# A four-stage LayerNorm and matmul kernel: the stores of prepared weight slabs are issued by SyncE in place of GpSimd

## The chip, the cores and the metric

The kernel runs on the eight cores of one Trainium2 chip. Every core runs the same program on its own 2048 rows of the activations; weights, mask and bias are the same for all. The metric is the device time in microseconds (us) of the slowest core. The kernel before takes 3483.27 us, the median of three runs (3479.4 to 3487.8).

A core has five instruction queues: TensorE (PE) for matmuls, VectorE (DVE), ScalarE (ACT), GpSimd (POOL) and SyncE (SP). Each runs its instructions in the order in which they are written and stops at a wait for a semaphore until that is reached. DMA transfers are issued by SP and by POOL here; SP's go through queue q1 of the profile, POOL's through q0.

## What is computed

```python
# x: (2, 8192, 4096) float32; weights (4096, 4096)
block_mask  = mask.reshape(128, 32, 128, 32).sum(axis=(1, 3)) > 0     # per 32x32 block
w_masked    = L0_attn_weight * repeat(repeat(block_mask, 32), 32)
x = x + layernorm(einsum('bsk,nk->bsn', layernorm(x), w_masked))      # layer 0
bin_weight  = sign(L0_ffn_weight)
x = x + layernorm(einsum('bsi,oi->bso', layernorm(x), bin_weight) + bias)   # layer 1
```

## The kernel before

**Tiling.** The 2048 rows of a core are worked in four chunks of 512 rows (loop over `c`), a chunk through layer 0 and then layer 1. A weight matrix is cut into 16 slabs of 2048 by 512 (`sl` from 0 to 15): slab `sl` has output columns of block `nsl = sl // 2` and the half `kh = sl % 2` of the inputs. A slab in bf16 is 2 MB and stands in one of two buffers WSL. For one slab TensorE does 64 matmuls (L465), 16 for each of the four row tiles.

**Chunk 0 prepares the weights.** The slabs come as float32 in eight quarters (name of the code; eight pieces of 512 KB) through two buffers WST: SP issues the load of piece `u` when piece `u - 2` has been used (L350 to L359). In layer 0 VectorE multiplies each piece by the block mask BTE and writes bf16 (L384); in layer 1 ScalarE takes the sign (L398). When all eight pieces of a slab are done, the slab is also written to DRAM (c1m, c2m; L405 to L413). Chunks 1 to 3 then load finished slabs of 2 MB from there on SP's queue (L424). A buffer WSL is written again only when the matmuls on it and its store are done (`free_marks`); chunk 1 waits for the store of the slab that it loads.

**The mask blocks.** In chunk 0, layer 0, the mask is reduced block by block (`emit_mask_chain(nsl)`, eight blocks, each for the two slabs of one `nsl`). POOL loads four pieces of 2 MB of the int32 mask (L240, into OS for even blocks and XP for odd ones), and halves each with five adds (L255). ScalarE copies the result to COLRED (L271), TensorE sums over partitions (L283), VectorE compares with zero (L297, "the mask step" below), TensorE transposes (L288), VectorE copies to BT (L301). POOL then sends BT to DRAM (btd, L314) and from there, replicated, to one of two BTE buffers (L323), after waiting that the multiplies with the block two before are done.

**What sets the order.** The order of the program text. Blocks 0 and 1 stand before everything else. In the loop over slabs, the preparation of slab `sl + 1` stands first, then the matmuls of slab `sl`, and after those of an even slab the mask block `sl // 2 + 2`. So VectorE has, in its order, the multiplies of slab 1, the mask step of block 2, the multiplies of slab 2, evictions, the multiplies of slab 3, the mask step of block 3, and so on. On POOL each store waits for the last multiply of its slab (`wt(g, ready)`).

The line in the loop that calls the function that is changed is `nxt = emit_w_load_prep(c, layer, sl + 1)`.

Of the kernel before, what the change touches and what calls it, by code (L numbers as in the profile page):

```python
# [37 lines left out]
def build():  # L38
# [11 lines left out]
    cm_d = [nc.dram_tensor("c1m", [NSL, 128, KTS * 512], BF16, kind="Internal"),  # L50
            nc.dram_tensor("c2m", [NSL, 128, KTS * 512], BF16, kind="Internal")]
# [3 lines left out]
    with es:  # L55
# [33 lines left out]
        def inc(ins, n, k=1):  # L89
            cnt[n] += k  # L90
            ins.then_inc(sem[n], k)
            return (n, cnt[n])

        def wt(eng, marker):
            if marker is None:
                return
            n, v = marker
            if v > 0:
                eng.wait_ge(sem[n], v)

        blk = es.enter_context(nc.Block())
# [227 lines left out]
        def emit_w_load_prep(c, layer, sl):  # L329
            su = state["slab_uses"]  # L330
            state["slab_uses"] += 1
            buf = WSL[su % 2]
            nsl, kh = sl // 2, sl % 2
            free_marks = []
            if su >= 2:
                free_marks.append(slab_done.get(su - 2))
                free_marks.append(cachew_use.get(su - 2))

            if c == 0:
                q_load = {}  # L340
                L1B = NSL * NQ

                @blk.sync
                def _(s):
                    for q in range(NQ):
                        u = state["wst_uses"]
                        state["wst_uses"] += 1
                        prior = u - 2
                        if prior >= 0:
                            if prior >= L1B:  # L350
                                s.wait_ge(sem["vW2"], prior - L1B + 1)
                            else:
                                s.wait_ge(sem["vW"], prior + 1)
                        sn = "sW%d" % (u % 2)
                        s.dma_start(WST[u % 2][:, :],
                                    (w1s_d if layer == 0 else w2s_d)[
                                        sl, :, q * 1024:(q + 1) * 1024]
                                    ).then_inc(sem[sn], 16)
                        cnt[sn] += 16  # L359
                        q_load[q] = (sn, cnt[sn])  # L360
                wfirst = state["wst_uses"] - NQ

                res = {}
                if layer == 0:
                    @blk.vector
                    def _(v):
                        for q in range(NQ):
                            wt(v, q_load[q])
                            if q == 0:
                                wt(v, bte_ready[nsl])  # L370
                                for fm in free_marks:
                                    wt(v, fm)
                            j0 = q * KTQ
                            dst = buf[:, j0 * 512:(j0 + KTQ) * 512].rearrange(
                                "p (j nb i) -> p j nb i", j=KTQ, i=32)
                            src = WST[(wfirst + q) % 2][:, :].rearrange(
                                "p (j nb i) -> p j nb i", j=KTQ, i=32)
                            mk = BTE[nsl % 2][:, (kh * 16 + j0) * 16:
                                              (kh * 16 + j0 + KTQ) * 16
                                              ].rearrange("p (j nb) -> p j nb",  # L380
                                                          j=KTQ
                                              ).unsqueeze(3).broadcast_to(
                                              [128, KTQ, 16, 32])
                            ins = v.tensor_tensor(dst, src, mk, op=OP.mult)  # L384
                            inc(ins, "vW", 1)
                        res["m"] = ("vW", cnt["vW"])
                        if kh == 1:
                            bte_freed[nsl] = ("vW", cnt["vW"])
                else:
                    @blk.scalar  # L390
                    def _(s):
                        for q in range(NQ):
                            wt(s, q_load[q])
                            if q == 0:
                                for fm in free_marks:
                                    wt(s, fm)
                            j0 = q * KTQ
                            ins = s.activation(buf[:, j0 * 512:(j0 + KTQ) * 512],  # L398
                                               WST[(wfirst + q) % 2][:, :], AF.Sign)
                            inc(ins, "vW2", 1)  # L400
                        res["m"] = ("vW2", cnt["vW2"])

                ready = res["m"]

                @blk.gpsimd  # L405
                def _(g):
                    wt(g, ready)
                    sn = "sC%d" % (su % 2)
                    g.dma_start(cm_d[layer][sl, :, :], buf[:, :]
                                ).then_inc(sem[sn], 16)  # L410
                    cnt[sn] += 16
                    cachew_use[su] = (sn, cnt[sn])
                    cachew_data[(layer, sl)] = (sn, cnt[sn])  # L413
            else:
                res = {}

                @blk.sync
                def _(s):
                    for fm in free_marks:
                        wt(s, fm)  # L420
                    if c == 1:
                        wt(s, cachew_data[(layer, sl)])
                    sn = "sWs%d" % (su % 2)
                    s.dma_start(buf[:, :], cm_d[layer][sl, :, :]  # L424
                                ).then_inc(sem[sn], 16)
                    cnt[sn] += 16
                    res["m"] = (sn, cnt[sn])
                ready = res["m"]

            return ready, su  # L430
# [366 lines left out]
        for c in range(NCH):  # L797
# [11 lines left out]
            for layer in range(2):  # L809
# [21 lines left out]
                for sl in range(NSL):  # L831
# [10 lines left out]
                    ready, su = pend  # L842
# [60 lines left out]
```

## Time and profile before

| | before |
|---|---|
| median of 3 runs | 3483.27 us |
| the profiled execution, its time | 3484.26 us |
| its span (core 1, the slowest of 3453.5 to 3482.7) | 3482.7 us |
| TensorE matmul busy | 2034.3 us (58%) |
| VectorE, ScalarE, GpSimd busy | 807.0, 607.7, 342.5 us |
| moved by DMA | 573.14 MB, mean 165 GB/s |
| granted TensorE clock, mean of a core | 0.809 to 0.816 |

"Span" is from the first to the last instruction of a core, so a little under the time of the execution. "Busy" is the time in which an engine worked on an instruction; an engine that is idle waited for something, and the views of waits say for what. The page's chain that ended last gives 37% of the span to TensorE and 33% to DMA; the latter is mostly loads of w1s, w2s and mask, all in chunk 0. In the page's 40 slices TensorE is busy for 1 to 3 tenths up to slice 12 and for 5 to 9 tenths after slice 14. So the first third of the span is a stage of another kind than the rest, and is read by itself.

### The profile page before, as it was taken

The numbers are of one execution on the slowest core, as the hardware profiler recorded it, in microseconds if no ns is written. First come the engines' busy times: TensorE is split into PE (matmuls) and PEld (weight loads), VectorE is DVE, ScalarE is ACT, GpSimd is POOL, SyncE is SP. The second block draws the span as 40 slices with busy tenths as digits, with TensorE's granted clock in tenths as the row PEclk, the third lists the DMA queues.
The fourth block names the chain that finished last, engine by engine and source line by source line (L and its number), as shares of the span: only waits on it lengthen the run. The fifth ranks groups of instructions, "written<-read, shape, count | busy, mean of one in ns | idle before, by whom it ended". The sixth has DMA issues, their size and how long they took to land.

```text
span 3482.7 us, 24252 instructions; the slowest of 8 cores (3453.5 to 3482.7 us)
## 1 busy us (share of the span) xinstructions
PE 2034.3 (58%) x9272; PEld 935.0 (27%) x9272; DVE 807.0 (23%) x1300; ACT 607.7 (17%) x460; POOL 342.5 (10%) x328
## 2 busy tenths in 40 slices
PE   1031233123351555556696599669759966974992
PEld 0020011001121222223243344324334432432441
DVE  0041222122233010104202322420232242013124
ACT  0130000000006333333011500301150030115000
POOL 3404223422300000000000000000000000000000
PEclk9995666566675787777898699889879987997996
DMA  3354655465562776774443244444324434442442
GB/s 121 102 181 169 212 181 171 165 213 180 167 216 73 231 229 224 244 241 176 174 158 145 99 161 176 142 176 165 146 97 154 184 135 179 145 165 77 146 153 113
DMA packets 72946, 573.14 MB, mean 165 GB/s; under 512 B 8800, under 2 KB 8816, under 8 KB 42112
## 3 DMA queue, kind: packets, MB, share of 16 engines
q1 hardware_dynamic: 54144, 377.51, 32.5%
q0 software_dynamic: 18688, 194.08, 14.8%
q8 instruction: 75, 1.23, 0.1%
q14 instruction: 39, 0.32, 0.0%
HBM read 470.86 MB, written 100.70 MB: 164 GB/s over the span
## 4 chain that ended last, share of the span: by engine, by line
PE 37%; DMA 33%; DVE 10%; ACT 10%; POOL 4%; issue 4%; DVEq 0%; SPq 0%; ACTq 0%; POOLq 0%
PE pmm L465 35%; DMA WST<-w2s 10%; DMA WST<-w1s 8%; DMA OS<-mask 4%; DMA XP<-mask 4%; DMA out<-OS 3%; DVE WSL L384 2%; POOL XP L255 2%; POOL MHI L255 2%; ACT WSL L398 2%; DMA XS<-x 2%; ACT HS L729 2%; ACT HS L698 2%; DVE OS L777 2%; ACT HT L214 1%
## 5 line engine op out<-in xcount | busy, mean ns | idle before, releaser
L465 PE MATMUL pmm<-WSL,HT 128*128 128x512 bf16 x8192 | 1904.8, 397 | 430.7 <-ACT WSL L398 196.5
L465 PEld LDWEIGHTS pmm<-WSL,HT 128*128 128x128 bf16 x8192 | 827.2, 102 | 1499.0 <-issue 620.7
L283 PE MATMUL ptB<-COLRED,P4T 128*4 128x512 bf16 x8 | 4.7, 584 | 581.3 <-ACT COLRED L271 581.3
L521 DVE TENSOR_TENSOR ARAW<-pmm,BIASF 128x512 bf16<-128x512 f32 x128 | 88.3, 692 | 896.6 <-PE pmm L465 896.6
L204 PE MATMUL ptA<-IDN,HS 128*128 128x128 bf16 x576 | 64.7, 302 | 349.9 <-ACT HS L729 236.0
L384 DVE TENSOR_TENSOR WSL<-WST,BTE 128x1024 bf16<-128x1024 f32 x128 | 156.0, 1224 | 210.1 <-DMA WST<-w1s 208.6
L502 DVE BATCH_NORM_STATS2 BNST<-ARAW 128x6 f32<-128x512 bf16 x96 | 59.3, 680 | 537.1 <-ACT ARAW L492 537.1
L398 ACT ACTIVATE WSL<-WST 128x1024 bf16<-128x1024 f32 x128 | 135.1, 1056 | 251.6 <-DMA WST<-w2s 251.4
L283 PEld LDWEIGHTS ptB<-COLRED,P4T 128*4 128x4 bf16 x8 | 0.6, 80 | 585.7 <-issue 585.7
L204 PEld LDWEIGHTS ptA<-IDN,HS 128*128 128x128 bf16 x576 | 56.6, 140 | 363.1 <-issue 362.4
L271 ACT ACT_TABLE_LOAD x8 | 10.3, 1283 | 822.4 <-POOL MHI L255 414.7
L255 POOL TENSOR_TENSOR XP<-XP 128x2048 int32<-128x2048 int32 (+4 forms) x80 | 120.6, 1508 | 103.6 <-DMA XP<-mask 95.8
L297 DVE TENSOR_SCALAR BRT<-ptB 4x512 bf16<-4x512 f32 x8 | 5.4, 679 | 517.5 <-PE ptB L283 517.5
L666 POOL DMA_DIRECT2D XS<-x x32 | 21.5, 673 | 1018.9 <-DVE XP L691 968.3
L214 ACT ACTIVATE HT<-ptA 128x2048 bf16<-128x2048 bf16 x36 | 67.6, 1877 | 274.1 <-PE ptA L204 274.1
L584 DVE BATCH_NORM_STATS2 BNST<-XS 128x6 f32<-128x512 f32 x128 | 78.4, 680 | 144.4 <-DMA XS<-x 144.4
L492 ACT ACTIVATE ARAW<-pmm 128x512 bf16<-128x512 f32 x96 | 57.3, 597 | 269.9 <-PE pmm L465 153.1
L492 ACT ACT_TABLE_LOAD x24 | 30.8, 1283 | 398.2 <-PE pmm L465 398.2
L528 DVE BATCH_NORM_STATS2 BNST<-ARAW 128x6 f32<-128x512 bf16 x160 | 98.9, 681 | 4.1
L553 POOL DMA_DIRECT2D XS<-x x24 | 12.7, 529 | 614.4 <-ACT HS L618 564.6
L777 DVE SCALAR_TENSOR_TENSOR OS<-XP,AUX,OS 128x4096 f32<-128x4096 bf16 x16 | 71.8, 4485 | 1.7
L255 POOL TENSOR_TENSOR MHI<-OS 128x2048 int32<-128x2048 int32 x16 | 57.5, 3595 | 97.4 <-DMA OS<-mask 97.4
(59 smaller groups left out, 813.3 us busy)
## 6 DMA issues: line engine op xcount, KB each, us to landing
WSL<-c1m SPq DMA_DIRECT2D x48, 2048.0 KB, 8.5
WSL<-c2m SPq DMA_DIRECT2D x48, 2048.0 KB, 7.9
WST<-w1s SPq DMA_DIRECT2D x128, 512.0 KB, 4.7
WST<-w2s SPq DMA_DIRECT2D x128, 512.0 KB, 4.9
XS<-x POOLq DMA_DIRECT2D x56, 1024.0 KB, 5.9
OS<-mask POOLq DMA_DIRECT2D x16, 2048.0 KB, 8.6
XP<-mask POOLq DMA_DIRECT2D x16, 2048.0 KB, 8.5
c1m<-WSL POOLq DMA_DIRECT2D x16, 2048.0 KB, 10.6
```

The costliest lines, as they stand in the source:

```text
L204: ins = t.transpose(pt[:, j * 128:(j + 1) * 128], HS[:, ktg * 128:(ktg + 1) * 128], IDN[:, :])
L214: ins = eng.activation(dst, src, AF.Identity)
L255: ins = g.tensor_tensor(tree[:, dst_off:dst_off + dst_n], a[:, :, 0], a[:, :, 1], op=OP.add)
L384: ins = v.tensor_tensor(dst, src, mk, op=OP.mult)
L398: ins = s.activation(buf[:, j0 * 512:(j0 + KTQ) * 512], WST[(wfirst + q) % 2][:, :], AF.Sign)
L465: ins = t.matmul(acc_bank(use8, nsl, tt), st_ap, mv_ap, start=(kh == 0 and j == 0), stop=(kh == 1 and j == KTS - 1))
L492: ins = s.activation(dst, acc_bank(use8, nsl, tt), AF.Identity)
L521: ins = v.tensor_tensor(dst, acc_bank(use8, nsl, tt), BIASF[:, nsl * 512:(nsl + 1) * 512], op=OP.add)
L528: ins = v.bn_stats(BNST[:, sslot * 48 + nsl * 6: sslot * 48 + (nsl + 1) * 6], ARAW[:, tt * D + nsl * 512: tt * D + (nsl + 1) * 512])
L584: ins = v.bn_stats(bn[:, (hf * 4 + q) * 6: (hf * 4 + q + 1) * 6], xb[:, q * 512:(q + 1) * 512])
L698: ins = s.activation(HS[:, :], XP[:, tt * D:(tt + 1) * D], AF.Square, accum_out=XSQ[:, tt:tt + 1])
L777: ins = v.scalar_tensor_tensor(OS[:, :], XP[:, tt * D:(tt + 1) * D], mrs3, OS[:, :], OP.subtract, OP.add)
```

## The change

The store of a prepared slab is issued by SP in place of POOL. It waits for the same thing, writes the same bytes from the same buffer and raises the same semaphore.

```diff
-                @blk.gpsimd
-                def _(g):
-                    wt(g, ready)
+                @blk.sync
+                def _(s):
+                    wt(s, ready)
                     sn = "sC%d" % (su % 2)
-                    g.dma_start(cm_d[layer][sl, :, :], buf[:, :]
+                    s.dma_start(cm_d[layer][sl, :, :], buf[:, :]
                                 ).then_inc(sem[sn], 16)
```

This moves 32 stores, 16 of each layer, from one queue to another. On TensorE, VectorE and ScalarE nothing moves.

POOL, between the end of mask block 1 and the start of block 2; lines with a minus stood there before, and "waits" gives the semaphores (vW counts multiplies):

```order
 L323 DMA BTE1<-btd 32x32x16 [waits sB]
 L323 DMA BTE1<-btd 32x32x16 x3
-L405 UNCONDITIONAL_BRANCH
-L409 DMA c1m<-WSL0 128x8192 [waits vW]
-L405 UNCONDITIONAL_BRANCH
-L409 DMA c1m<-WSL1 128x8192 [waits vW]
 L231 UNCONDITIONAL_BRANCH
 L240 DMA OS<-mask 128x4096
```

The BTE transfers of one block and the mask loads of the next are now neighbours; the same holds at each later block.

SP before, at the end of slab 0 and the start of slab 1 of w1s:

```order
L355 DMA WST0<-w1s 128x1024 [waits vW]
L355 DMA WST1<-w1s 128x1024 [waits vW]
L343 UNCONDITIONAL_BRANCH
L355 DMA WST0<-w1s 128x1024 [waits vW]
L355 DMA WST1<-w1s 128x1024 [waits vW]
```

SP now, at the same place:

```order
L355 DMA WST0<-w1s 128x1024 [waits vW]
L355 DMA WST1<-w1s 128x1024 [waits vW]
L405 UNCONDITIONAL_BRANCH
L409 DMA c1m<-WSL0 128x8192 [waits vW]
L343 UNCONDITIONAL_BRANCH
L355 DMA WST0<-w1s 128x1024 [waits vW]
L355 DMA WST1<-w1s 128x1024 [waits vW]
```

The store stands between the last load of a slab and the first of the next, in layer 0 and, with ScalarE's count vW2, in layer 1.

## Rows read from the trace of the kernel before

**Rows 1.** Stages of core 1: from:to, length, busy of each engine, PEclk, DMA share, GB/s

```profile
268.00:914.00 646.00, 166.11 (x669) 68.74 (x670) 126.23 (x131) 11.47 (x12) 218.69 (x180) 0.62 0.54 181
...
1134.00:1565.00 431.00, 240.56 (x961) 100.46 (x962) 43.08 (x74) 152.63 (x142) 9.04 (x17) 0.77 0.72 234
```

**Rows 2.** Waits of the whole span: us in total, times, longest

```profile
DVE BRT L297 <- PE ptB L283: 517.5, 8, 65.9
...
POOL c1m L409 <- DVE WSL L384: 413.5, 16, 74.0
```

**Rows 3.** Timeline of 610 to 740: start, us, engine, line, operation, idle before

```profile
670.07 8.10 POOL L255 TENSOR_TENSOR XP<-XP 128x2048 int32<-128x2048 int32 x5 [3.65 <-DMA XP<-mask]
...
681.47 0.68 DVE L297 TENSOR_SCALAR BRT<-ptB 4x512 bf16<-4x512 f32 x1 [65.51 <-PE ptB L283]
...
686.43 3.14 POOL L323 DMA_DIRECT2D BTE<-btd  x4 [2.36 <-issue]
...
703.23 1.23 DVE L384 TENSOR_TENSOR WSL<-WST,BTE 128x1024 bf16<-128x1024 f32 x1 [2.11 <-DMA WST<-w1s]
...
731.98 1.23 DVE L384 TENSOR_TENSOR WSL<-WST,BTE 128x1024 bf16<-128x1024 f32 x1 [2.70 <-DMA WST<-w1s]
733.76 0.55 POOL L409 DMA_DIRECT2D c1m<-WSL  x1 [28.17 <-DVE WSL L384]
734.31 0.53 POOL L240 DMA_DIRECT2D OS<-mask  x1
```

**Rows 4.** Timeline of VectorE, mask steps of blocks 2 and 7

```profile
333.05 0.68 DVE L297 TENSOR_SCALAR BRT<-ptB 4x512 bf16<-4x512 f32 x1 [65.60 <-PE ptB L283]
...
913.11 0.68 DVE L297 TENSOR_SCALAR BRT<-ptB 4x512 bf16<-4x512 f32 x1 [65.31 <-PE ptB L283]
```

**Rows 5.** Chain that ended last, pieces in order of time: start, us, what

```profile
617.07 14.61 DMA XP<-mask
...
636.06 8.31 DMA XP<-mask
...
1203.70 9.20 DMA WST<-w2s
```

**Rows 6.** Line L409, stores of layer 1: duration in ns, first and last start

```profile
L409 POOL DMA_DIRECT2D c2m<-WSL x16: 531/531/538, 1152.0 to 1565.2; - x16
...
DMA to landing us min/median/max: 9.1/10.5/12.4
```

**Rows 7.** Timeline of ScalarE, signs of one slab in layer 1

```profile
1224.54 1.06 ACT L398 ACTIVATE WSL<-WST 128x1024 bf16<-128x1024 f32 x1 [1.91 <-DMA WST<-w2s]
...
1229.81 1.06 ACT L398 ACTIVATE WSL<-WST 128x1024 bf16<-128x1024 f32 x1 [1.49 <-DMA WST<-w2s]
```

**Rows 8.** Timeline of 150 to 300, around the first store

```profile
163.84 3.15 POOL L323 DMA_DIRECT2D BTE<-btd  x4 [1.74 <-DMA btd<-BT]
...
240.96 0.57 POOL L409 DMA_DIRECT2D c1m<-WSL  x1 [73.97 <-DVE WSL L384]
...
266.22 1.22 DVE L384 TENSOR_TENSOR WSL<-WST,BTE 128x1024 bf16<-128x1024 f32 x1 [1.69 <-DMA WST<-w1s]
```

**Rows 9.** Chain that ended last, in chunk 1

```profile
1645.09 14.38 DMA out<-OS
```

**Rows 10.** Line L424, the one load issued in 1644 to 1645

```profile
L424 SPq DMA_DIRECT2D WSL<-c1m x1: 320/320/320, 1644.7 to 1644.7; - x1
...
DMA to landing us min/median/max: 10.0/10.0/10.0
```

**Rows 11.** DMA issues of the whole span: count, KB each, median us to landing

```profile
out<-OS SPq DMA_DIRECT2D x16, 2048.0 KB, 7.1
```

**Rows 12.** Timeline of TensorE, first matmuls of chunk 1

```profile
1585.67 5.30 PE L465 MATMUL pmm<-WSL,HT 128*128 128x512 bf16 x16 [3.10 <-ACT HT L214]
```

**Rows 13.** DMA of 1200 to 1500: 40 slices of 7.5 us, and issues

```profile
GB/s 233 316 180 186 323 225 208 170 391 201 150 273 232 194 192 317 200 200 181 385 146 174 216 300 158 199 274 369 262 198 255 317 168 181 336 183 180 163 410 142
...
WST<-w2s SPq DMA_DIRECT2D x86, 512.0 KB, 4.9
```

## The prediction, made before the changed kernel was run

> **What bounds the kernel now.** I read the page's parts 4 and 5 first, then the stages, then the waits, then one round of the first chunk instruction by instruction. Times are of core 1, the slowest. The diff touches chunk 0 only, whose layer 1 ends near 1565 us; from there on the kernel loads finished slabs. In the stages [rows 1] the reader sees that 268 to 914 has TensorE busy for 166 of 646 us at 181 GB/s: this stretch is bound by neither matmuls nor transfers. The waits say what holds it [rows 2]: VectorE waits 517.5 us in eight waits for TensorE's mask matmul (L283, read by L297), and POOL's queue waits 413.5 us in sixteen waits for VectorE's multiplies before it issues a store of a finished slab (L409). The two wait for each other.
>
> One round shows the ring [rows 3]. At 733.76 POOL issues the store of the round's second slab, just after VectorE's last multiply (731.98). Only then, at 734.31, does it issue the first load of the next mask block. While POOL reduces a block VectorE is idle: its next instruction in order is the mask step, here at 681.47, and the 16 multiplies of the next two slabs stand behind that. So a round is a sum: 51.7 us from the mask step (681.47) to the last multiply's end (733.2), then the mask part. The mask step of block 2 starts at 333.05 and that of block 7 at 913.11 [rows 4]: five rounds of 116.0 us.
>
> **The change, part by part.**
>
> *Taken from POOL: 32 store issues with their waits.* The issues (0.55 us each) are nothing; the waits are the matter. Without them POOL runs from a block's BTE transfers straight into the next block's loads. It can be one block ahead: its own BTE step waits for VectorE's mask step, and the multiplies that free BTE stand ahead of that in VectorE's order. So the round becomes the longer of two loops.
>
> Loop A, POOL. From the mask step to the end of the BTE issues 8.1 us (681.47 to 689.57) [rows 3]. Then four rows of the block, each a load of length L; after each of the first three 4.4 us up to the next load's issue (631.7 to 636.06 [rows 5]), after the last 8.1 us of adds (670.07 to 678.17 [rows 3]) and 3.3 us to the mask step. Together 4L + 8.1 + 13.2 + 8.1 + 3.3 = 4L + 32.7. L is 8.3 us when nothing else moves and 14.6 us behind a store on its own queue [rows 5]. The nearest row to a 2 MB transfer of POOL's queue beside the weights is the store of layer 1: 9.1 to 12.4 us, median 10.5 [rows 6]. I take 11: loop A is 77 us (ends 66 and 91).
>
> Loop B, VectorE: 51.7 us for two slabs with the mask transfers absent, plus what these cost the quarters. The price of a 2 MB transfer beside the weights is in layer 1: a slab takes 27.5 us (store issues at 1152.0 and 1565.2 [rows 6], 15 slabs between them), while undisturbed quarters follow each other every 2.65 us (1224.54 and 1229.81, one between [rows 7]), 21.2 us for eight; so 6.3 us. About three of the four loads fall on the multiplies: 19 us. Then a thing that no row shows: the multiply reads two tensors of SBUF beside POOL's adds, which now run at the same time. Ends: nothing, and all of POOL's adds of a block, 4 x 8.1 = 32 us. I take 9 us, near the lower end, since POOL adds for only some 30 of 80 us and the multiplies mostly wait for data: 16 multiplies, times 0.38, times 1.5 us, the mean length of an add. Loop B is then 80 us (ends 52 and 51.7 + 25.2 + 32 = 109).
>
> On that last term the Trainium skill speaks against the change: "SBUF — State Buffer", section "Who interferes with whom", says that a VectorE instruction with two SBUF inputs contends with a GpSimd instruction that reads SBUF, and that the second to issue blocks fully until the first is done. No run here shows it; by that rule the multiplies do lose time, the zero end is out, and the sum keeps its term.
>
> The longer loop gives a round of **80 us**, with ends 66 and 109.
>
> *Where the rounds start.* Mask block 1's BTE issues end at 167 us and POOL then idles 74 us until the first store [rows 8]. Now it starts block 2 there, and is done with it by about 167 + 4 x 11 + 13.2 + 8.1 = 232, before VectorE is. So mask step 2 comes at the end of slab 1's multiplies, 267.4 (266.22 + 1.22), plus delay: three pairs of x loads beside mask loads, 2.7 us each as L gains (11 against 8.3), 8; and one mask load beside the weights, 6. That is 281, say 280. Mask step 7 comes at 280 + 5 x 80 = 680 instead of 913: **233 us gained** (ends: 275 + 5 x 66 = 605, gain 308; 285 + 5 x 109 = 830, gain 83). What follows block 7 is late next: four slabs, the handover to layer 1, layer 1.
>
> *Put on SP's queue: 32 stores, each between the eighth load of a slab and the first of the next.* Two costs. SP now waits for the last multiply (or sign) before it can issue the next slab's first quarter, which before needed only the seventh. And that quarter stands behind 2 MB on the same queue. Two 2 MB transfers that SP issued at 1644.7 and 1645.1 landed 4.8 us apart, after 10.0 us (1654.7) and 14.38 us (1659.5) [rows 9, 10]; a quarter of that size is 1.2 us. A 2 MB store on SP takes 7.1 us [rows 11]. From the last sign of a slab: 0.4 issue, 7.1 store, 1.2 for the first quarter, 1.2 for the second, 1.1 for its sign: 11.0, then six quarters at 2.65: 26.9 us per slab, against 27.5 now. The store already costs the loads as much beside them as it would ahead of them. I take **nothing** for the 18 boundaries that nothing hides (15 in layer 1, 3 after mask step 7). Ends: the store does not hold the loads at all, four pairs at 5.3 plus 1.1 = 22.3, -5.2 each, -94; and a store of 12.4 us (the slowest [rows 6]), 32.2, +4.7 each, +85. Within the rounds the boundary is in loop B: 11.0 + 6 x 2.9 = 28.4 against the 28.7 from 704.5 (703.23 + 1.23) to 733.2, no change.
>
> *Free:* the x loads of the second half of layer 0 and of chunk 1 come sooner on POOL, but those wait for normalisations, not for POOL. Slab 0 of chunk 1 is now issued behind the last store on SP, near 1565.5, and lands by 1565.5 + 7.1 + 4.8 = 1577; its first matmul starts at 1585.67 [rows 12]. Eight us of cover; without it the cost would be 12. From chunk 1 on nothing else moves.
>
> **Sum.** The profiled execution took 3484.3 us (span 3482.7), 1 us above the median of 3483.3. 3484.3 - 233 + 0 = 3251; as a median **3250 us**.
>
> **The rivals.**
>
> *Transfer rate as floor.* A round moves 4 x 2.1 + 16 x 0.524 + 2 x 2.1 = 21.0 MB; in 80 us that is 262 GB/s on all cores at once, and neither stage of [rows 1] is above 234. At 234 the round is 90 us: step 7 at 280 + 450 = 730, gain 183, **3300 us**. Against it: layer 1's quarters wait for their buffers, and slices of 7.5 us reach 391 and 410 GB/s [rows 13]. The Trainium skill ("SBUF — State Buffer", "A bandwidth-pool intuition that's wrong") gives about 358 GB/s of HBM per core; by that the floor would be an estimated 59 us and the forecast would stand.
>
> *More comes.* Mask loads stay near 8.3 us and the store does not hold the loads: 3484 - 308 - 94 = 3082 with all of it; with half of the surplus over the forecast, **3165**.
>
> *The stores do not let go.* POOL is held to the same place by another wait (BTE free, COLRED, or the mask step), so that the change does not decouple anything and the round stays 116: **3483**. Against it: in VectorE's order all of these come before its idle stretch [rows 4].
>
> *Slower: weights lose their turn.* With mask loads nearly always in flight each of the 16 quarter loads becomes like the one that met a store, 9.20 us [rows 5], instead of the median 4.9 [rows 13]: pairs of 11 us, 88 for two slabs, 18 behind stores and 5 of evictions, 111, plus 9 for the adds: 120 per round, so step 7 at 880, and the boundaries at +85: 3484 - 33 + 85 = **3536**. It decides from rounds of 110 us on (280 + 5 x 110 + 85 = 915). Against it: beside a 2 MB store of now only one or two of eight quarters are long, as the median shows.
>
> **How the numbers follow.** Forecast (both loops overlap, about 80 us) 0.66; floor 0.20; more 0.07; no effect 0.03; slower 0.04. Range 3170 to 3340: it holds the forecast with rounds from 70 to 90 us and boundaries up to +40, and the floor. Faster by over 0.2% (7 us, about what can be told from no change) 0.93, same 0.03, slower 0.04.
>
> **What would show it.** Right: mask steps 2 and 7 near 280 and 680; POOL's first mask load of a block right behind BTE issues; mask loads near 11 us; VectorE's idle before L297 down from 65 to under 15 us; layer 1 still about 431 us, and everything from 1565 on shifted only. Wrong: a round above 95 us, layer 1 longer than 470 us, or mask loads that start only after the multiplies.

## The result: 2.7% faster, two fifths of the gain forecast

The changed kernel takes 0.9728 of the time of the kernel before (95% interval 0.9695 to 0.9762), some 3389 us against 3483. Forecast were 3250, with 3170 to 3340 as the range. So the sign is right, and 94 us came where 233 were expected.

In the profiled execution after, cores 0 to 5 had a lower granted clock (0.789 to 0.804) than cores 6 and 7 (0.809 and 0.807) and took 37 to 116 us longer than these, so the rows below are of core 7 in both traces (3453.8 us before, 3375.1 us after). Stages of core 7 before, then after; columns as in [rows 1]:

```profile
324.00:902.00 578.00, 165.51 (x666) 68.36 (x665) 125.16 (x130) 9.56 (x10) 185.82 (x155) 0.63 0.56 183
902.00:1008.00 106.00, 64.50 (x262) 27.12 (x263) 49.48 (x50) 0.00 (x0) 5.60 (x9) 0.81 0.67 214
1136.00:1542.00 406.00, 238.54 (x961) 99.67 (x960) 43.05 (x74) 146.31 (x136) 9.04 (x17) 0.80 0.73 240
```

```profile
281.00:736.00 455.00, 175.80 (x665) 70.78 (x665) 199.62 (x131) 9.56 (x10) 208.53 (x145) 0.64 0.72 232
736.00:861.00 125.00, 72.76 (x261) 28.96 (x262) 49.33 (x51) 0.00 (x0) 4.82 (x7) 0.69 0.68 219
993.00:1461.00 468.00, 264.99 (x960) 105.82 (x960) 43.19 (x74) 144.47 (x136) 0.00 (x0) 0.70 0.65 202
```

The stages are the five rounds from mask step 2 to mask step 7, the four slabs behind them, and 15 slabs of layer 1. The first shrank by 123 us. The second grew by 19 and the third by 62, the latter at 202 GB/s in place of 240: together they give back two thirds of that. VectorE is busy for 200 us in the rounds in place of 125 with the same work.

The mask steps of blocks 2 and 7 after, as in [rows 4]:

```profile
281.87 0.67 DVE L297 TENSOR_SCALAR BRT<-ptB 4x512 bf16<-4x512 f32 x1
...
736.01 0.67 DVE L297 TENSOR_SCALAR BRT<-ptB 4x512 bf16<-4x512 f32 x1
```

The first is where it was forecast (280; core 1, from which the forecast was made, has 283.7), and no wait stands behind either: VectorE's 65 us of idle are gone. But a round takes 90.8 us, not 80. Sum on core 7 at the last store: mask step 7 came 166 us sooner (902.1 to 736.0), minus 19 for the four slabs, 4 for the handover and 62 for layer 1 leaves 81 us sooner (1542.3 to 1461.1); the trace after is already some 5 us late at the mask steps of blocks 0 and 1.

### The profile page after: what moved, and what is told of

It is laid out like the page before. It is cut to its first block, busy times and chain, and to the rows that moved or that the text cites. A ratio compares the mean times of both kernels' runs of the same rounds, so it can differ in the third digit from the quotient of the medians.

```text
span 3491.2 us, 24252 instructions; the slowest of 8 cores (3375.1 to 3491.2 us)
## 1 busy us (share of the span) xinstructions
PE 2157.5 (62%) x9272; PEld 964.1 (28%) x9272; DVE 881.6 (25%) x1300; ACT 606.2 (17%) x460; POOL 354.4 (10%) x296
## 4 chain that ended last, share of the span: by engine, by line
PE 40%; DMA 32%; DVE 11%; ACT 10%; issue 4%; POOL 1%; SPq 0%; DVEq 0%; ACTq 0%; POOLq 0%
PE pmm L465 38%; DMA WST<-w1s 13%; DMA WST<-w2s 10%; DVE WSL L384 4%; DMA out<-OS 3%; ACT WSL L398 2%; DMA XS<-x 2%; ACT HS L729 2%; ACT HS L698 2%; DVE OS L777 2%; ACT HT L214 1%; DVE BNST L584 1%; DMA OS<-mask 1%; DMA WSL<-c1m 1%; PE ptA L204 1%
## 5 line engine op out<-in xcount | busy, mean ns | idle before, releaser
L465 PE MATMUL pmm<-WSL,HT 128*128 128x512 bf16 x8192 | 2027.5, 416 | 626.0 <-ACT WSL L398 242.2
L465 PEld LDWEIGHTS pmm<-WSL,HT 128*128 128x128 bf16 x8192 | 855.3, 105 | 1788.1 <-issue 1212.1
L521 DVE TENSOR_TENSOR ARAW<-pmm,BIASF 128x512 bf16<-128x512 f32 x128 | 88.5, 691 | 1069.0 <-PE pmm L465 1069.0
L384 DVE TENSOR_TENSOR WSL<-WST,BTE 128x1024 bf16<-128x1024 f32 x128 | 229.0, 1807 | 371.8 <-DMA WST<-w1s 340.4
L255 POOL TENSOR_TENSOR XP<-XP 128x2048 int32<-128x2048 int32 (+4 forms) x80 | 137.5, 1719 | 109.6 <-DMA XP<-mask 101.9
L255 POOL TENSOR_TENSOR MHI<-MHI 128x1024 int32<-128x1024 int32 (+1 forms) x64 | 75.6, 1181 | 7.7
L255 POOL TENSOR_TENSOR MHI<-OS 128x2048 int32<-128x2048 int32 x16 | 57.5, 3596 | 104.4 <-DMA OS<-mask 104.4
L774 DVE TENSOR_SCALAR OS<-ARAW,RS 128x4096 f32<-128x4096 bf16 x16 | 37.6, 2353 | 117.8 <-DMA out<-OS 116.8
## 6 DMA issues: line engine op xcount, KB each, us to landing
XP<-mask POOLq DMA_DIRECT2D x16, 2048.0 KB, 10.6
```

The source lines that it names most:

```text
L255: ins = g.tensor_tensor(tree[:, dst_off:dst_off + dst_n], a[:, :, 0], a[:, :, 1], op=OP.add)
L465: ins = t.matmul(acc_bank(use8, nsl, tt), st_ap, mv_ap, start=(kh == 0 and j == 0), stop=(kh == 1 and j == KTS - 1))
L521: ins = v.tensor_tensor(dst, acc_bank(use8, nsl, tt), BIASF[:, nsl * 512:(nsl + 1) * 512], op=OP.add)
```

## The experiments

Three theories had to be told apart. Freed chain: POOL's wait tied the mask blocks to the slabs. Boundary: each store on SP's queue costs the loads behind it, by its place in line or by the wait in front of it. For the round of 90.8 us: multiplies that are held until an add of POOL's is done (lock), or transfers at their rate (21.0 MB in 90.8 us is 231 GB/s, close to the 234 that a rival had named as floor).

| kernel | ratio to before, interval | round | slab of layer 1 |
|---|---|---|---|
| before | 1 | 116.0 (115.4 to 117.5) | 27.4 (27.1 to 27.7) |
| the change | 0.9728 (0.9695 to 0.9762) | 92.0 and 90.8 | 31.5 and 31.2 |
| l0_only | 0.9617 (0.9553 to 0.9681) | 92.3 (89.9 to 93.5) | 27.5 (27.0 to 28.4) |
| act_queue | 0.9453 (0.9419 to 0.9487) | 89.2 (88.6 to 89.6) | 27.0 (26.5 to 27.7) |
| pool_waits | 1.0286 (1.0250 to 1.0321) | 118.4 (117.9 to 119.2) | 31.6 (31.0 to 32.1) |
| store_later | 0.9495 (0.9458 to 0.9531) | 89.1 (87.8 to 90.4) | 27.1 (26.8 to 27.3) |
| mask_in_psum | 0.9370 (0.9325 to 0.9415) | 82.1 (79.6 to 84.0) | 27.2 (26.6 to 28.0) |
| sp_waits_only | 0.9717 (0.9692 to 0.9742) | 92.0 (90.8 to 94.0) | 31.2 (30.2 to 31.8) |
| psum_and_sp | 0.9621 (0.9596 to 0.9647) | 83.7 (82.6 to 85.5) | 30.9 (30.2 to 31.4) |
| before_sp_waits | 1.0215 (1.0159 to 1.0271) | 119.6 (118.7 to 121.2) | 29.0 (28.6 to 29.5) |
| store_after_one | 0.9512 (0.9481 to 0.9543) | 89.0 (88.3 to 89.4) | 27.0 (26.5 to 27.5) |
| psum_store_later | 0.9409 (0.9386 to 0.9431) | 82.8 (80.4 to 86.6) | 27.1 (26.9 to 27.4) |
| no_layer0_stores | 0.9213 (0.9188 to 0.9237) | 76.0 (75.0 to 77.2) | 26.7 (26.3 to 27.0) |

"Round" is a fifth of the time from mask step 2 to mask step 7, "slab" a fifteenth of that from the first to the last store of layer 1, in us, in the profile of each: the mean of the eight cores with the lowest and the highest in brackets, and for the change cores 6 and 7. The cores of one kernel differ by 1 to 6 us in the round and by up to 1.6 us in the slab, so a difference of one core to one core that is no larger says nothing. The expectations below quote single cores.

**The store issues on POOL or its waits?** The wait alone was put back:

```diff
                     cachew_data[(layer, sl)] = (sn, cnt[sn])
+                @blk.gpsimd
+                def _(g):
+                    wt(g, ready)
```

> The changed kernel, with POOL still waiting for the last multiply or sign of each slab where it waited before, but issuing nothing there. Theory A (the wait, not the issue, tied the mask chain to the slabs): rounds go back to 116 us and more (two stores in line, 8 us per round), mask steps 2 to 7 in 610 to 620 us instead of 454, and the boundaries keep their 80 us: about 3484 + 80 + 40 = 3600, slower than the kernel before. Rival (POOL's store issues or its queue were the cost, not the wait): stays near 3390.

3579 us in place of the 3600 expected, rounds of 118.4. The timeline of POOL in that kernel shows one boundary:

```profile
697.55 2.34 POOL L323 DMA_DIRECT2D BTE<-btd  x3 [0.18 <-issue]
744.13 0.57 POOL L240 DMA_DIRECT2D OS<-mask  x1 [44.24 <-DVE WSL L384]
```

POOL stands for 44 us in front of the next block's load, as it did in [rows 3] in front of the store. The whole gain of the change is this wait, and not the store's queue.

**Layer 0 alone.** The stores of layer 0 stay on SP's queue, those of layer 1 go back to POOL's: `@(blk.sync if layer == 0 else blk.gpsimd)` in place of `@blk.sync`, with two more semaphores:

> [...] Theory A (the gain is the mask chain set free, and every store in front of the next slab's first quarter costs what layer 1 shows, 31.2 against 27.1 us a slab): layer 1 back to 27.1 a slab, 62 us less than the changed kernel, about 3325. Theory B (layer 1 is slower because transfers run at their rate and the shift in time only moves the cost): layer 1 stays near 31, about 3390. Mask rounds stay at 90.8 either way.

3336 us, layer 1 at 27.5 a slab: the loss in layer 1 belongs to the store's move there, and the move had nothing to give there.

**A third queue.** `@blk.scalar` in place of `@blk.sync`:

> All 32 stores issued by ScalarE, so neither POOL waits for multiplies nor does a store stand in front of loads on SP's queue. Theory A: layer 1 at 27.1 a slab (-62 against the changed kernel), four slabs after mask step 7 at 26.5 (-19), and rounds shorter than 90.8: two boundaries of 4 us each less, 82 to 85 us, -35: about 3275. Theory B (rounds of 90.8 us are the rate floor: 21 MB at 231 GB/s): rounds stay at 90 or more, only what lies behind them gains, about 3310 or above.

3291 us: both losses behind the rounds are gone (four slabs 106.9 us on core 4, layer 1 27.0 a slab). The rounds went only to 89.2, 2 to 3 us less, not to 82 to 85, so most of what they are too long has another cause than the boundary. ScalarE's queue is not free of cost in the rounds either: its store waits for the last multiply, and the copy to COLRED of the next mask block stands behind it, so the mask step now finds VectorE idle for 3.5 us per round (17.6 us in five waits, core 4).

**Wait or place in line?** First the store behind the next slab's first two quarters on SP (`STORE_AT = 2`), then behind the first (`STORE_AT = 1`):

```diff
                     for q in range(NQ):
+                        if q == STORE_AT and pend_store:
+                            pend_store.pop(0)(s)
```

> The changed kernel with each store on SP's queue placed behind the first two quarters of the next slab instead of in front of them. SP then does not wait for the last sign before the first quarter, and two quarters are in before the store. Theory A (place in line is the cost): layer 1 from 31.2 to 23 to 26 us a slab (-80 to -120 against the changed kernel), rounds to about 82 us (-40), four slabs after step 7 -20: about 3230. Theory B (rate): no slab under 27 and no round under 90, about 3330 or above.

> The changed kernel with each store behind the first quarter of the next slab: that quarter keeps its head start (it is issued after the seventh multiply), the second stands behind the 2 MB. Wait theory: the head start is worth most of the 4 us, so 28 to 29 us a slab in layer 1 and about 3320 in all. Line theory: a quarter behind the store costs as before, 30 to 31 a slab, about 3370.

3300 and 3304 us. The gain over the change is there (27.1 a slab), but the 23 to 26 us a slab that I expected did not come, and with only one quarter ahead of the store it is the same 27.0. So a quarter right behind 2 MB costs nothing that the kernel does not pay anyway. Then the wait alone, with the store on ScalarE's queue, and once in the kernel before, with its stores on POOL:

```diff
+                @blk.sync
+                def _(s):
+                    wt(s, ready)
-                @blk.sync
+                @blk.scalar
                 def _(s):
                     wt(s, ready)
                     sn = "sC%d" % (su % 2)
```

> Stores on ScalarE's queue, but SP still waits for the last multiply or sign of a slab before the first load of the next, as in the changed kernel. Splits the boundary's 4.1 us: if the wait is the price, layer 1 is near 31 us a slab; if the 2 MB in line are the price, it stays near 27.6. I expect between, nearer to the line: 28.5, so 3290 + 15 x 0.9 + 10 = 3315.

> The kernel before (stores on POOL's queue, POOL's waits as they were), and SP waits for the last multiply or sign of each slab before the first load of the next. Wait theory (the price of the changed kernel's boundaries is SP's wait, which takes the first quarter's head start and makes it meet the store): layer 1 from 27.5 to 30.2 us a slab (+40), slabs after mask step 7 +12, rounds 116 to 119 (+15): about 3484 + 67 = 3550, slower. Line theory (2 MB ahead in SP's queue): no change, 3484.

My expectation of the first, "nearer to the line", failed: 31.2 us a slab and 3383 us, slab and time of the changed kernel (31.2 and 31.5; ratios 0.9717 and 0.9728), though no store stands in SP's queue. So the wait alone makes the whole 4 us by which a slab is above act_queue's 27.0, and the place in line adds nothing that can be told from zero. In the second the wait costs the kernel before 2.2% (1.6 to 2.7; 3554 us, expected 3550). There a slab grows by 1.6 us, from 27.4 to 29.0: beside a store that POOL issues the same wait costs less than half, and why is open. The timeline of the changed kernel shows what is lost (layer 1, core 7, ScalarE and SP):

```profile
1107.90 1.06 ACT L398 ACTIVATE WSL<-WST 128x1024 bf16<-128x1024 f32 x1 [1.40 <-DMA WST<-w2s]
1110.32 1.06 ACT L398 ACTIVATE WSL<-WST 128x1024 bf16<-128x1024 f32 x1 [1.37 <-DMA WST<-w2s]
1111.45 0.33 SPq L409 DMA_DIRECT2D c2m<-WSL  x1
...
1122.69 1.28 ACT L398 ACT_TABLE_LOAD   x1 [11.31 <-DMA WST<-w2s]
1123.98 2.00 ACT L398 ACTIVATE WSL<-WST 128x1024 bf16<-128x1024 f32 x2
```

No load is in flight when the last sign ends at 1111.4, since the quarter that could have gone at 1109.0 waited too. The two quarters are issued at 1111.9 and 1112.3 and land 10.6 and 11.4 us later, so at 1122.5 and 1123.7. ScalarE is idle for 11.3 us, then does its table load (1.28 us), and finds both quarters there. The same place in store_after_one:

```profile
1099.30 1.06 ACT L402 ACTIVATE WSL<-WST 128x1024 bf16<-128x1024 f32 x1 [1.83 <-DMA WST<-w2s]
1100.42 0.33 SPq L412 DMA_DIRECT2D c2m<-WSL  x1
1102.21 1.28 ACT L402 ACT_TABLE_LOAD   x1 [1.85 <-DMA WST<-w2s]
1103.50 1.06 ACT L402 ACTIVATE WSL<-WST 128x1024 bf16<-128x1024 f32 x1
1111.87 1.06 ACT L402 ACTIVATE WSL<-WST 128x1024 bf16<-128x1024 f32 x1 [7.31 <-DMA WST<-w2s]
```

The quarter with the head start is ready 1.85 us after the last sign, and the table load and a sign are done while the store goes out.

**Lock or rate?** The multiply's mask operand was moved from SBUF, the memory in which all buffers so far stand, to PSUM, the one that TensorE writes its results to (ScalarE copies each block from 2 on; stores on ScalarE's queue, in the second kernel on SP's):

```diff
+                    ins = s.activation(mask_ps(nsl), BTE[nsl % 2][:, :],
+                                       AF.Identity)
...
-                            mk = BTE[nsl % 2][:, (kh * 16 + j0) * 16:
+                            mt = BTE[nsl % 2][:, :] if nsl < 2 else mask_ps(nsl)
+                            mk = mt[:, (kh * 16 + j0) * 16:
```

> The kernel with the stores on ScalarE's queue, in which ScalarE also copies each mask block from 2 on from SBUF to PSUM, and the multiply reads the mask there: one SBUF input in place of two, the same bytes moved. Lock theory (multiplies that overlap POOL's adds are held until the add is done; mean 1.86 us instead of 1.22, 14 us per round): multiplies back at 1.22 to 1.25, rounds from 88.6 to 75, mask step 7 some 70 us earlier, about 3225. Rate theory (21 MB per round at 231 to 239 GB/s is what the transfers give): multiplies faster, rounds stay at 86 or more, their waits for w1s longer, about 3280.

> The changed kernel (stores on SP's queue) with the mask read from PSUM. Lock theory: rounds from 90.8 to about 77, mask step 7 at about 665, layer 1 unchanged at 31.2, so about 3320. Rate theory: rounds stay at 88 or more, 3380.

The multiplies in the rounds, one row each from the groups of instructions of before, of the change (both core 7), of act_queue and of mask_in_psum (from mask step 3 on, where all read PSUM); x, busy us, mean ns, idle before:

```profile
L384 DVE TENSOR_TENSOR WSL<-WST,BTE 128x1024 bf16<-128x1024 f32 x80 | 97.0, 1223 | 119.3 <-DMA WST<-w1s 118.4
```

```profile
L384 DVE TENSOR_TENSOR WSL<-WST,BTE 128x1024 bf16<-128x1024 f32 x80 | 170.7, 2156 | 252.3 <-DMA WST<-w1s 243.5 <-DMA btd<-BT 8.8
```

```profile
L384 DVE TENSOR_TENSOR WSL<-WST,BTE 128x1024 bf16<-128x1024 f32 x80 | 178.2, 2240 | 215.9 <-DMA WST<-w1s 215.2
```

```profile
L399 DVE TENSOR_TENSOR WSL<-WST,ptA 128x1024 bf16<-128x1024 f32 x64 | 77.7, 1220 | 187.4 <-DMA WST<-w1s 186.2 <-issue 0.4
```

From 1223 to 2156 ns and, with the mask in PSUM, back to 1220. The hold of the adds on the multiplies is real and is 14.7 us of VectorE's time per round ((170.7 - 97.0) / 5). Taking it off gives less than that: the four rounds that read PSUM take 82.4 us on core 4 (mean of the cores 80.3), 7 to 9 under act_queue's, not the 75 expected, and the kernel 3261 us where I expected 3225. The pure rate theory fails too, since that stretch moves more than any stage did before; stage 362 to 692 of mask_in_psum:

```profile
362.00:692.00 330.00, 134.13 (x522) 55.39 (x532) 100.53 (x105) 15.19 (x16) 144.39 (x116) 0.68 0.79 260
```

260 GB/s, where "floor" had taken 234. psum_and_sp has rounds of 81.7 us from mask step 3 on and 3351 us, above the 3320 expected.

The missing part is the other loop. In mask_in_psum VectorE is idle before the mask step again, which it was not in the changed kernel, while POOL waits only for the mask chain itself (core 4):

```profile
610.88 0.68 DVE L301 TENSOR_SCALAR BRT<-ptB 4x512 bf16<-4x512 f32 x1 [6.75 <-PE ptB L287]
612.97 0.56 POOL L320 DMA_DIRECT2D btd<-BT  x1 [5.10 <-DVE BT L305]
```

The 5.1 us are the way of a block from POOL's last add to VectorE's copy. VectorE's idle time is 9.8 us per round on core 4 (39.3 in four) and 6.6 to 10.8 on the others. Without it the round would be 72.6 us, so VectorE's loop did come down to about the 75 expected, and POOL's loop is now the longer one. The prediction's sum for it, 4L + 32.7 with the 12.1 us that a mask load takes there in the median, is 81.1 us, against 82.4 measured.

**What is left of the round.** mask_in_psum with the stores of layer 0 left out. Chunks 1 to 3 load layer 1's slabs in layer 0 too, so they move the same bytes, but their layer 0 does not get its own weights:

```diff
+                if layer == 1:
                     @blk.scalar
...
-                    s.dma_start(buf[:, :], cm_d[layer][sl, :, :]
+                    s.dma_start(buf[:, :], cm_d[1][sl, :, :]
```

> Stores on ScalarE's queue and mask in PSUM, but the 16 stores of layer 0 are left out, and chunks 1 to 3 load layer 1's slabs in their place (the same bytes). 16.8 instead of 21.0 MB in a round. Transfer theory (what is left of the round is transfers delaying each other): rounds from 82 to about 75, slabs after mask step 7 from 27 to 22: 3261 - 35 - 20 = 3205. Chain theory (loads wait for buffers, and adds, mask step and BTE stand in a row): rounds stay at 80 or more, about 3240.

3205 us as expected; the four rounds from mask step 3 on take 75.3 us in the mean of the cores, in place of 80.3. A fifth fewer bytes shorten the round by 5 us, at 224 GB/s on core 1, far under the 260, so the transfers are not at one fixed rate. POOL's loop is the longer one here too (VectorE idle before the mask step for 9 to 16 us per round), and what fewer transfers do is to shorten its mask loads, from a median of 12.1 us to 11.0: 4L + 32.7 is 76.7, and core 1 has 76.5.

**Both costs off on SP alone.**

> Mask read from PSUM and stores on SP's queue behind the first two quarters of the next slab: both costs of the changed kernel taken off at once without ScalarE's queue. If they add, about 3389 - 90 (store later) - 38 (PSUM) = 3261, layer 1 at 27.1, rounds of 81 to 82 us. If the round is by now set by POOL's loop, the place of the store changes nothing in it and the gain is layer 1's and the last four slabs' alone.

3272 us against the 3261 of the sum, so the gains add nearly in full in time. In the rounds the place of the store changes next to nothing (81.3 us from mask step 3 on, 81.7 in psum_and_sp), as expected of a round that POOL's loop sets; layer 1 goes from 30.9 to 27.1 a slab. Of the versions that compute the same as before, this one and mask_in_psum (0.9409 and 0.9370 of before) are the fastest, and their intervals overlap.

## Why the prediction failed, step by step

**What bounds the kernel: right.** The wait of POOL's queue closed the ring; pool_waits puts it back, and with it the rounds of 116 us and more.

**Where the rounds start: right.** POOL's first load of block 2 is issued at 166.85 and mask step 2 comes at 281.9, forecast 167 and 280.

**Loop A, POOL: not the longer, but longer than its sum.** Mask loads have a median of 10.8 us in the rounds of the change, forecast 11. POOL now waits for VectorE's mask step. Waits of POOL and VectorE in the rounds, core 7:

```profile
POOL btd L314 <- DVE BT L301: 91.6, 5, 54.6
```

```profile
DVE WSL L384 <- DMA WST<-w1s: 243.5, 55, 11.8
```

Of POOL's wait 54.6 us stand before the first round; the four others are 9.3 us each, and 5.1 of these pass in any case. So POOL had only 4 us to spare in a round of 90.8, and its loop was about 87 us, not 77. From the mask step to the next mask load it took 12 to 14.5 us in place of 8.1 (its wait for the btd transfer grew from about 2 us to 6.5 to 8.7), and the last row's adds some 10.6 us in place of 8.1. Why the small btd transfer took so long was not tested.

**Loop B, VectorE: mis-sized, 90.8 in place of 80 us.** Two terms of the sum failed. The adds' hold on the multiplies was taken at 9 us, by the chance of meeting times the mean length of an add; it is 14.7. The longest multiply took 4.6 us, its own 1.2 and nearly the whole of the largest add (3.6). The Trainium skill's rule ("SBUF — State Buffer", section "Who interferes with whom"), which the prediction could not show in a row, says that a VectorE instruction with two SBUF inputs contends with a GpSimd instruction that reads SBUF. The traces agree with it, down to that condition: with one of the two inputs in PSUM the multiplies are at 1220 ns beside the same adds. The second term is the quarters' wait: 19 us for the mask loads and nothing for the boundary. The rows say 26.6 us ((252.3 - 119.3) / 5), and in act_queue, without the boundary, 19.3 ((215.9 - 119.3) / 5). So the mask loads' price was right, and the boundary cost 7 us of waiting per round where "no change" stood. The round before without its 66.0 us of waiting for the mask step was 49.5 us; plus 14.7 and 26.6 that is 90.8. The same sum for act_queue, 49.5 + 16.2 + 19.3 and the 3.5 us before the mask step, is 88.5 against 88.6 measured on core 4: what its rounds won at the boundary they partly lost to ScalarE's queue.

**The stores on SP's queue: wrong, the step that failed most.** The sum gave "nothing" for 18 boundaries; the four slabs and layer 1 lost 19 + 62 = 81 us, close to the pessimistic end (+85), which the range did not reach down to. The prediction named both costs, the wait and the place in line, and summed them into 26.9 us a slab: second sign done 11.0 us after the last sign of the slab before, then six quarters at 2.65. In the change (core 7, mean over the slabs of layer 1) the second sign is done after 14.4 us and the six take 16.7, together 31.1. Of the 3.4 us that the first term is short, 2.4 are the landing of the first quarter (11.1 us after the last sign, forecast 8.7), and here the store's 7.1 us was too small: the stores of layer 1 on SP's queue land after 9.3 us in the median. The table load of 1.28 us was in no term. It is there before as well, but then one quarter is ready at 1.53 us and the table load is done while the others are on their way (the kernel before, core 7):

```profile
1243.09 1.28 ACT L398 ACT_TABLE_LOAD   x1 [1.53 <-DMA WST<-w2s]
```

The mechanism behind it was mis-stated: "a store ahead costs what a store beside costs". It does, with one quarter sent before it (store_after_one: 27.0 us a slab, the second sign done after 11.8). What costs is that no quarter is under way when the store starts, and sp_waits_only shows this to be the whole of the 4 us, with the store on another queue. That head start was named and never given a price.

**The rivals.** Rate as floor got the round right (90 us) for the wrong reason: 231 GB/s in the rounds, but 260 in mask_in_psum. "Weights lose their turn" named the right loop; the median quarter in the rounds went from 4.4 to 7.4 us, not to the 9.2 that the rival needed.

**The range.** 3389 lies 49 us above its upper end. The ends worked out for the terms (rounds to 109 us, boundaries to +85) held the result; the range took 90 and +40. The rounds alone used up their part (90.8), and the boundaries went 41 us beyond theirs. The signs of being wrong that the prediction set were not met (a round above 95 us, layer 1 above 470; it took 468), so they would not have told that the time falls outside the range.

## What to carry to other kernels

A wait on an in-order queue delays everything behind it. When an issue with a wait is moved from one queue to another, ask for each queue separately what the wait holds back: on POOL it was 66 us of mask work, on SP the head start of one load, 2.4 us early, worth 4 us a slab in layer 1. Put such an issue behind the next independent loads (store_after_one, store_later), or on a queue that has nothing to hold back (act_queue, where little stood behind it), and the freed chain comes without most of the loss. When two engines that took turns are made to overlap, price their meeting: the hold on the multiplies and the transfers' delay of each other took 14.7 and 19.3 us of each round here. And when one of two loops is made shorter, ask how much the other has to spare. It was 4 us here, and taking 14.7 us from VectorE's loop shortened the round by 7 to 9, so much only because POOL's last adds (back to 8.1 us) and its wait for btd (back to 1.7) became shorter with it.

## What the runs showed of the hardware

VectorE multiplies of 128x1024 with both inputs in SBUF took 2156 ns in the mean and up to 4617 ns beside GpSimd adds, 1223 ns without them and 1220 ns beside them with one input in PSUM. The large adds suffer less than the small ones: the 128x512 one went from 1037 to 1642 ns in the mean in the rounds (XP tiles), the 128x2048 one from 3596 to 3639.

With at least one quarter load issued before the last sign of the slab before, a 2 MB store costs a slab of layer 1 the same within 0.4 us on every queue: 27.4 (POOL's, before), 27.0 (ScalarE's), 27.1 and 27.0 (SP's, behind two and one quarter). With no load issued until that sign is done, a slab took 31.2 us with the store on SP's or on ScalarE's queue and 29.0 with it on POOL's.

The mean rate of a stage on all eight cores at once reached 260 GB/s per core (mask_in_psum, core 4, DMA share 0.79). Mask loads of 2 MB took 12.1 us there in the median, and 8.6 in the rounds of the kernel before (core 7).
